# Two-layer masked GNN on one core: layer 1's query and key weights multiplied with the map's on the chip, and part of a round's products moved into the next round

## The chip, the core and the metric

One core of a Trainium2 chip. TensorE multiplies into PSUM, VectorE and ScalarE take results out of PSUM, GpSimd works in SBUF, SyncE (SP) issues most DMAs. The metric is the device time of one execution in microseconds. The kernel before: 4122.58 us, median of 3 runs (4117.27 to 4124.95).

## The reference, cut to what matters

x has the shape (64, 256, 512): 64 graphs of 256 nodes; adj is a boolean mask (64, 256, 256). Graphs don't depend on each other.

```python
# layer 0: 4 heads of 64
h = maximum(layernorm(x), 0)
q, k, v = h @ Wq, h @ Wk, h @ Wv
x = x + softmax(where(adj, q @ k.T / 8, -max)) @ v @ Wo + bo
# layer 1: 8 heads of 64
h = maximum(layernorm(x), 0)
m = h @ map_w.T + map_b
q, k = m @ q_w.T + q_b, m @ k_w.T + k_b
n = m / norm(m per head)
cos_adj = (n @ n.T, zero where adj) > 0.1
p = softmax(where(adj, -1e10, q @ k.T / 8)) * keep
a = cos_adj * p
out = relu(a @ (h @ gcn_map.T + gcn_map_b) @ gcn_W.T / (a.sum(-1) + 1))
x = x + out
```

## The kernel before, in words

All is kept in SBUF for one graph at a time; weights are loaded once. Most products are made of three fp32r matmuls: each operand is held as a high part (rounded to fp32r) and a low part (the rest), and `PASSES` multiplies high by high, high by low and low by high. The high part is written by ScalarE from PSUM, the low part by VectorE (PSUM less the high part). Transposes, the products with attention weights and the sums of squares are plain fp32.

The work is software-pipelined over rounds. `rounds` calls a body with (a, n): in one round the heads' part of layer 1 of graph a, and all else for graph n = a + 1. The first round has only n, the last only a; 63 rounds have a new graph behind the first. The order of each engine inside a round is a written list, one per engine: `TENSOR`, `SCALAR`, `VECTOR`, `POOL`, `SYNC` (from L50 on). An engine runs its list strictly in order, with semaphore waits. Strings are steps of graph n, tuples (with a pair number 0 to 3) steps of graph a.

Steps of graph n: `ht0a/b` transposes h of layer 0 (hT high and low); `qk0` to `qk3` project q, k; `v0` projects v; `s0` to `s3` are scores of four heads, followed by exp on ScalarE, `sum` (GpSimd scales prob, L417); `pt` transposes prob; `av` multiplies with v; `wo0/1` is the output projection, after which VectorE makes x_mid and its statistics (L663, L533, L540), GpSimd rstd (L359, L362) and VectorE h (`norm1`, L546). `ht1a/b` transposes it. `m0` to `m3` are the map. ScalarE writes qkm high, VectorE m32 (L670) and qkm low (L671). `q0`..`q3` and `k0`..`k3` project q and k from qkm; `vv0/1` is the value product with a weight `w_v` which the kernel makes itself in the first round (`fold`: gcn_map times gcn_W). `ss` sums squares of m, GpSimd raises them to -1/2 (`pow`, L441), `rt` transposes and `bc0/1` spread them over partitions; VectorE scales m32 (L699).

Steps of graph a, for each pair of heads: `unit` (nrm high L518, low L402), `score`, `cos`, ScalarE's exp (L475), VectorE's mask and gate (L607, L618), `turn_a/b` (transposes to uT, L481), `value` (L783), `back` (transposes; VectorE L634, GpSimd adds to x_res, L410).

PSUM has 8 banks: 0 to 3 belong to the pairs' steps, 4 to 7 go round the string steps in TENSOR's order (`bank_of`). `empty` makes TensorE wait until the previous user of a bank has been taken out.

Of the kernel before, what the change touches and what calls it, by code (L numbers as in the profile page):

```python
# [23 lines left out]
def gnn_two_layers(nc, x, adj, wq, wk, wv, wo, bo, map_t, map_b, q_t, q_b, k_t, k_b, gcn_map, gcn_map_b, gcn_t, out):  # L24
# [3 lines left out]
    DH = 64  # L28
# [75 lines left out]
    with ctx:  # L104
# [28 lines left out]
        hT = sb("hT", [128, 2, KT, N], F32R)  # L133
        qkm = sb("qkm", [128, 2, KT, N], F32R)
# [7 lines left out]
        q1 = sb("q1", [128, 2, KT, N], F32R)  # L142
        k1 = sb("k1", [128, 2, KT, N], F32R)
# [7 lines left out]
        gcn_rows = att[:, :, :, :, :].rearrange("p a b c n -> p (a b c n)").rearrange("p (h d) -> p h d", d=D)  # L151
        rel = sb("rel", [128, C, 128])
# [43 lines left out]
        fold_done = count("fold_done")  # L196

# [8 lines left out]
        pT_ready = count("pT_ready")  # L206

# [67 lines left out]
        SPLIT_HIGH = at(SCALAR, ("qk0", "qk2", "exp0", "exp1", "pt0", "pt2"), 4)  # L275
        SPLIT_LOW = at(VECTOR, ("qk1", "qk3", "sum0", "sum1", "av", "wo0"), 4)
        FOLD = at(TENSOR, ("s2", "pt0", "av", "wo0", "ht1a"), 0)
        FOLD_HIGH = at(SCALAR, ("exp3", "pt1", "av", "ht1a"), 0)
        FOLD_LOW = at(VECTOR, ("sum3", "av", "wo0", "ht1a", "ht1b"), 0)
# [3 lines left out]
        def _(sp):  # L283
            with nc.allow_non_contiguous_dma("small biases, once"):
                sp.dma_start(x_in[:, :, :], x[0].rearrange("(c p) d -> p c d", p=128)).then_inc(x_loaded, 16)
                sp.dma_start(adj8[:, :, :], adj[0].rearrange("(c p) j -> p c j", p=128)).then_inc(adj_loaded, 16)
# [8 lines left out]

            def body(a, n, more):
                for s in steps(SYNC, a, n, more):
                    kind, p = s if isinstance(s, tuple) else (s, None)
                    if kind == "x":
# [5 lines left out]
                        sp.dma_start(x_in[:, :, :], x[n + 1].rearrange("(c p) d -> p c d", p=128)).then_inc(x_loaded, 16)  # L305
                    elif kind == "out":
# [4 lines left out]
                    elif kind == "move":  # L311
# [21 lines left out]
        def _(pool):  # L333
# [44 lines left out]
            def body(a, n, more):  # L378
                for s in steps(POOL, a, n, more):
# [66 lines left out]
        def _(act):  # L446
# [13 lines left out]
            def body(a, n, more):  # L460
                for s in steps(SCALAR, a, n, more):
# [3 lines left out]
                    if a is None and kind in FOLD_HIGH:  # L465
                        kt = FOLD_HIGH[kind]
                        act.wait_ge(fold_full, kt + 1)
                        s_.activation(w_v[:, 0, kt, :], bank[kt][:, :], ACT.Copy).then_inc(fold_hi, 1)
# [17 lines left out]
                    elif kind[:2] == "ht":  # L486
                        t = 2 * "ab".index(kind[3])
                        act.wait_ge(product_full, in_psum(n, kind))
                        s_.activation(flat(hT[:, 0, t:t + 2, :]), bank[bank_of[kind]][:, :], ACT.Relu).then_inc(high_done, 1)
# [19 lines left out]
                    elif kind[0] in "mqk" and kind[1].isdigit():  # L509
                        t = int(kind[1])  # L510
                        dst, bias = {"m": (qkm, bias_m), "q": (q1, bias_q), "k": (k1, bias_k)}[kind[0]]
# [3 lines left out]
                        s_.activation(dst[:, 0, t, :], bank[bank_of[kind]][:, 0:N], ACT.Identity, bias=bias[:, t:t + 1]).then_inc(high_done, 1)  # L515
# [4 lines left out]
            rounds(act, body)  # L520

        @block.vector
        def _(dve):
# [404 lines left out]
```

## Time and profile before

| | |
|---|---|
| median of 3 runs | 4122.58 us |
| profiled execution, its own time | 4121.26 us |
| its span, first to last instruction | 4119.5 us |
| TensorE matmul busy | 3931.4 us, 95% |
| TensorE weight loads | 3437.0 us, 83% |
| VectorE / ScalarE / GpSimd busy | 63% / 48% / 32% |
| mean granted TensorE clock | 0.993 of full |
| the chain that ended last | TensorE 65%, VectorE 12%, issue 11%, ScalarE 6%, GpSimd 4% |

How to read it: busy time of TensorE overlaps itself, since matmuls are pipelined and their ends are modelled; times from one group's start to the next one's start are surer. A fp32 matmul is listed as two records, a transpose as one. "Idle before" names what ended the idle time ahead of an instruction.

### The profile page before, as it was taken

How to read it: one execution, taken by the hardware profiler on the slowest of the kernel's cores; microseconds unless marked ns; L12 is line 12 of the kernel's file. 1: busy time of each engine (PE TensorE's matmuls, PEld its weight loads, DVE VectorE, ACT ScalarE, POOL GpSimd, SP SyncE). 2: the span in 40 equal slices, each digit the busy share in tenths (PEclk: the TensorE clock that was granted, in tenths of full speed). 3: DMA queues.
4: the chain of work that ended last, by engine and by line, in shares of the span. 5: the costliest groups of instructions: out<-in, count | busy, mean ns of one | idle time of the engine just before them, and what ended most of it. 6: DMA issues, size and time to landing. Idle time of an engine off the chain costs nothing.

```text
span 4119.5 us, 105002 instructions
## 1 busy us (share of the span) xinstructions
PE 3931.4 (95%) x32976; PEld 3437.0 (83%) x32976; DVE 2608.3 (63%) x9426; ACT 1979.3 (48%) x5583; POOL 1324.3 (32%) x2007
## 2 busy tenths in 40 slices
PE   7999999999999999999999999999999999999997
PEld 6888888888888888888888888888888888888886
DVE  4666666666666666666666666666666666666664
ACT  3554544544545445445454454454454544544544
POOL 3333333333332333333333333333333333333332
PEclk8999999999999999999999999999999999999998
DMA  3000000000000000000000000000000000000000
GB/s 87 16 32 26 22 32 16 32 32 16 32 27 21 32 18 30 32 16 32 29 18 32 22 25 32 16 32 32 16 32 27 21 32 16 32 32 16 32 27 17
DMA packets 65544, 111.77 MB, mean 27 GB/s; under 512 B 20880, under 2 KB 22448, under 8 KB 65520
## 3 DMA queue, kind: packets, MB, share of 16 engines
q1 hardware_dynamic: 64928, 110.12, 7.8%
q0 software_dynamic: 592, 1.35, 0.2%
q8 instruction: 13, 0.21, 0.0%
q14 instruction: 11, 0.09, 0.0%
HBM read 44.34 MB, written 33.55 MB: 19 GB/s over the span
## 4 chain that ended last, share of the span: by engine, by line
PE 65%; DVE 12%; issue 11%; ACT 6%; POOL 4%; DVEq 1%; DMA 1%; POOLq 0%; ACTq 0%; SPq 0%
PE bank L755 34%; PE bank L763 9%; PE bank L748 7%; PE bank L783 6%; PE bank L775 4%; ACT prob L501 3%; PE bank L883 3%; POOL prob L417 2%; DVE x_mid L663 2%; ACT att L475 2%; DVE prob L650 2%; DVE att L607 2%; DVE att L618 1%; POOL rstd L362 1%; DVE hT L640 1%
## 5 line engine op out<-in xcount | busy, mean ns | idle before, releaser
L475 ACT ACTIVATE att<-att,nmax 128x256 f32<-128x256 f32 x1024 | 509.7, 500 | 299.6 <-DVE nmax L607 299.6
L417 POOL TENSOR_SCALAR prob<-prob,rsum 128x256 f32<-128x256 f32 x512 | 241.1, 487 | 631.2 <-DVE rsum L657 628.2
L755 PE MATMUL bank<-hT,w_qkv 128*128 128x256 f32 x3072 | 414.9, 288 | 4.7 <-DVE hT L640 4.7
L755 PE MATMUL bank<-qkm,w_k 128*128 128x256 f32 x3072 | 416.6, 285 | 0.0
L755 PEld LDWEIGHTS bank<-hT,w_qkv 128*128 128x128 f32 x3072 | 376.9, 189 | 37.9 <-issue 24.2
L755 PE MATMUL bank<-hT,w_map 128*128 128x256 f32 x3072 | 396.7, 285 | 5.1 <-DVE hT L640 1.0
L618 DVE SCALAR_TENSOR_TENSOR att<-bank,att 128x256 f32<-128x256 f32 x1024 | 392.3, 420 | 4.0
L755 PE MATMUL bank<-qkm,w_q 128*128 128x256 f32 x3072 | 390.8, 283 | 0.0
L755 PEld LDWEIGHTS bank<-hT,w_map 128*128 128x128 f32 x3072 | 372.5, 189 | 18.4 <-DVE hT L640 17.3
L763 PE MATMUL bank<-w_v,hT 128*128 128x512 f32 x1536 | 385.3, 399 | 0.0
L755 PEld LDWEIGHTS bank<-qkm,w_k 128*128 128x128 f32 x3072 | 380.1, 188 | 5.0
L481 ACT ACTIVATE uT<-bank 128x512 f32<-128x512 f32 x512 | 292.2, 598 | 181.1 <-PE bank L748 169.5
L515 ACT ACTIVATE q<-bank,bias_q 128x256 fp32r<-128x256 f32 x256 | 121.0, 473 | 537.1 <-PE bank L755 535.2
L607 DVE CUSTOM_DVE_ANT_0 att<-bank,mask 128x256 f32<-128x256 f32 x1024 | 372.1, 420 | 7.3 <-PE bank L775 2.3
L755 PEld LDWEIGHTS bank<-qkm,w_q 128*128 128x128 f32 x3072 | 373.4, 189 | 0.1
L763 PEld LDWEIGHTS bank<-w_v,hT 128*128 128x128 f32 x1536 | 278.6, 188 | 82.6 <-issue 24.2
L783 PE MATMUL bank<-uT,v 128*64 128x256 f32 x2048 | 280.1, 395 | 49.4 <-ACT uT L481 49.4
L410 POOL TENSOR_TENSOR x_res<-x_res,rel 128x256 f32<-128x256 f32 x256 | 189.0, 738 | 420.4 <-DVE rel L634 420.4
L689 DVE SCALAR_TENSOR_TENSOR q<-bank,bias_q,q 128x256 fp32r<-128x256 f32 x256 | 117.1, 478 | 321.4 <-ACT q L515 321.4
L359 POOL TENSOR_SCALAR var_e<-mv 128x2 f32<-128x2 f32 x128 | 24.7, 193 | 913.9 <-DVE mv L540 913.9
L634 DVE SCALAR_TENSOR_TENSOR rel<-bank,fac 128x256 f32<-128x256 f32 x256 | 108.7, 424 | 314.6 <-PE bank L820 310.1
L515 ACT ACTIVATE k<-bank,bias_k 128x256 fp32r<-128x256 f32 x256 | 121.5, 474 | 373.9 <-PE bank L755 373.9
(122 smaller groups left out, 7949.6 us busy)
## 6 DMA issues: line engine op xcount, KB each, us to landing
x_in<-x SPq DMA_DIRECT2D x64, 512.0 KB, 3.4
x_res<-x_mid SPq DMA_DIRECT2D x64, 512.0 KB, 3.1
out<-x_res SPq DMA_DIRECT2D x64, 512.0 KB, 2.8
adj<-adj SPq DMA_DIRECT2D x64, 64.0 KB, 2.6
att<-gcn_map POOLq DMA_DIRECT2D x2, 512.0 KB, 9.0
x_mid<-wq SPq DMA_DIRECT2D x1, 512.0 KB, 5.6
x_res<-wk SPq DMA_DIRECT2D x1, 512.0 KB, 6.8
v<-wv SPq DMA_DIRECT2D x1, 512.0 KB, 7.7
```

The costliest lines, as they stand in the source:

```text
L410: g.tensor_tensor(part, part, rel[:, :, :], ALU.add).then_inc(res_added, 1)
L417: last = g.tensor_scalar(prob0[:, hd, c, :], prob0[:, hd, c, :], rsum0[:, hd, c:c + 1], 0.0, ALU.mult, ALU.add)
L475: s_.activation(e_sl, e_sl, ACT.Exp, bias=nmax1[:, p, c, e:e + 1], scale=-1.0, accum_out=esum1[:, p, c, e:e + 1]).then_inc(exp1_done, 1)
L481: s_.activation(uT[:, e, :], t_bank[e][:, :], ACT.Copy).then_inc(uT_ready, 1)
L515: s_.activation(dst[:, 0, t, :], bank[bank_of[kind]][:, 0:N], ACT.Identity, bias=bias[:, t:t + 1]).then_inc(high_done, 1)
L607: v_.tensor_tensor_reduce(out=att[:, p % 2, e, c, :], in0=score_bank[e][:, c * N:c * N + N], in1=mask1[:, c, :], scale=-SCALE, scalar=FLT_ ...
L618: v_.scalar_tensor_tensor(e_sl, gram_bank[e][:, c * N:c * N + N], COS_THRESHOLD, e_sl, ALU.is_gt, ALU.mult, accum_out=usum1[:, p, c, e:e + ...
L748: last = t_.transpose(dst[:, b * 128:b * 128 + 128], src_of(outer, c), ident[:, :])
L755: last = t_.matmul(dst, w(ws, k)[:, t * 128:t * 128 + 128], rhs[:, rs, k, :], start=(k == 0 and i == 0), stop=(k == KT - 1 and i == 2))
L763: last = t_.matmul(dst, lhs[:, ls, k, c * 128:c * 128 + 128], w(ws, k), start=(k == 0 and i == 0), stop=(k == chunks - 1 and i == 2))
L775: last[e] = t_.matmul(banks[e][:, c * N:c * N + N], left[r, ls, c * 128:c * 128 + 128], right[r, rs, :], start=(i == 0), stop=(i == 2))
L783: last = t_.matmul(dst[64 * e:64 * e + 64, :], v[:, jc, (hd0 + e) * DH:(hd0 + e + 1) * DH], rhs(e, jc), start=(jc == 0), stop=(jc == C - 1))
```

## The change

1. q and k of layer 1 no longer come from m but from h directly: in the first round the kernel multiplies q_t and k_t with the map's weights (8 folds of 4 fp32 matmuls of 128x512) and their bias (2 folds of 16 matmuls of one column), takes the results out as high and low parts, and adds the bias. The raw weights (`q_raw`, `k_raw`, `map_raw`) are loaded to slots that are free then. The value weight's folds stay.
2. m is only needed in fp32: ScalarE writes m32, VectorE has no operation for m.
3. `q`, `k` of pairs 2 and 3 and both value products are made in the next round, as steps of graph a: `("k", 2)`, `("q", 2)`, `("k", 3)`, `("q", 3)`, `("vv", 0)`, `("vv", 1)`. q1, k1 hold two pairs in place of four.
4. The transposed h of layer 1 has a buffer of its own, gT, as it must live into the next round.
5. All five orders are written anew. `empty` now knows products of both kinds.

```diff
     TENSOR = [
-        "ht0a", ("score", 0), "ht0b", ("cos", 0), "qk0", "qk1", ("turn_a", 0), "qk2", ("turn_b", 0), "s0", "s1", ("value", 0),
-        "qk3", ("back", 0), ("score", 1), ("cos", 1), "s2", "s3", "pt0", "v0", "pt1", ("turn_a", 1), ("turn_b", 1), "pt2",
-        "pt3", ("value", 1), "av", ("back", 1), ("score", 2), ("cos", 2), "wo0", "wo1", ("turn_a", 2), ("turn_b", 2),
-        ("value", 2), ("score", 3), ("back", 2), "ht1a", "ht1b", ("cos", 3), "m0", "m1", "m2", ("turn_a", 3), ("turn_b", 3),
-        "m3", ("value", 3), "vv0", "ss", "q2", "q1", "q0", "k1", ("back", 3), "rt", "k0", "q3", "k3", "bc0", "bc1", "k2",
-        "vv1"
+        ("vv", 0), "ht0a", ("score", 0), ("cos", 0), ("vv", 1), ("turn_a", 0), "ht0b", ("k", 2), ("turn_b", 0), "qk0",
+        ("value", 0), ("score", 1), "qk1", "qk2", "qk3", ("back", 0), "s0", "s1", ("cos", 1), "s2", "s3", "v0", "pt0",
+        ("turn_a", 1), ("turn_b", 1), "pt1", "pt2", ("q", 2), "pt3", ("value", 1), "av", ("back", 1), ("score", 2), ("cos", 2),
+        "wo0", "wo1", ("k", 3), ("turn_a", 2), ("turn_b", 2), ("q", 3), ("value", 2), "ht1a", "ht1b", ("back", 2),
+        ("score", 3), ("cos", 3), "m0", "m1", "m2", "m3", "q0", ("turn_a", 3), "ss", ("turn_b", 3), "k0", ("value", 3), "rt",
+        "q1", "bc1", "bc0", "k1", ("back", 3)
     ]
...
     VECTOR = [
...
+        ("vv", 0), ("score_a", 0), "ht0a", ("score_b", 0), ("cos_a", 0), ("cos_b", 0), "ht0b", ("vv", 1), ("factor", 0),
+        ("score_a", 1), "qk0", ("k", 2), ("score_b", 1), "qk1", "qk2", ("back", 0), "qk3", "s0", ("cos_a", 1), "s1", "sum0",
+        "s2", ("cos_b", 1), "sum1", "s3", "sum2", "v0", "sum3", ("q", 2), ("factor", 1), ("back", 1), "av", ("score_a", 2),
+        ("score_b", 2), ("cos_a", 2), "wo0", ("cos_b", 2), "wo1", ("k", 3), "norm1", ("factor", 2), ("q", 3), ("back", 2),
+        "ht1a", "ht1b", "stats0", ("score_a", 3), ("score_b", 3), ("cos_a", 3), ("cos_b", 3), "ss", "q0", "k0", "rt", "norm0",
+        ("factor", 3), "bc0", "q1", ("back", 3), "bc1", "k1"
     ]
     POOL = [
...
+        ("unit", 0), ("unit", 1), "mid", "mask0", ("back", 0), "sum0", "sum1", "sum2", "sum3", ("back", 1), "rstd1",
+        ("back", 2), "rstd0", "m0", "m1", "m2", "m3", "pow", "mask1", ("back", 3)
     ]
     SYNC = [
-        "x", ("out", 0), "move", "adj"
+        "x", ("out", 0), "adj", "move"
     ]
...
-        q1 = sb("q1", [128, 2, KT, N], F32R)
-        k1 = sb("k1", [128, 2, KT, N], F32R)
+        q1 = sb("q1", [128, 2, 2, N], F32R)
+        k1 = sb("k1", [128, 2, 2, N], F32R)
...
+        gT = sb("gT", [128, 2, KT, N], F32R)
...
-                    elif kind in ("m0", "m1", "m2", "m3"):
-                        t = int(kind[1])
-                        v_.tensor_scalar(m32[:, t, :], full[:, 0:N], bias_m[:, t:t + 1], None, ALU.add)
-                        v_.scalar_tensor_tensor(qkm[:, 1, t, :], full[:, 0:N], bias_m[:, t:t + 1], qkm[:, 0, t, :].bitcast(F32),
-                                                ALU.add, ALU.subtract).then_inc(product_done, 1)
...
+                if f in (BIAS_Q, BIAS_K):
...
+                    for t in range(KT):
+                        for k in range(KT):
+                            last = t_.matmul(full[:, t:t + 1], raw(k)[:, t * 128:t * 128 + 128], bias_m[:, k:k + 1], start=(k == 0), stop=(k == KT - 1))
+                else:
+                    t = f - (QUERY_W if query else KEY_W)[0]
+                    for k in range(KT):
+                        last = t_.matmul(full[:, :], map_raw[:, k, t * 128:t * 128 + 128], raw(k), start=(k == 0), stop=(k == KT - 1))
...
+                    if kind in ("q", "k", "vv"):
+                        pe.wait_ge(product_done, out_of_psum(a, "ht1b"))
+                        empty(a, n, s)
+                        if kind == "vv":
+                            last = project_rows(full[:, :], gT, KT, p, lambda s2, k: w_v[:, s2, k, :])
                         else:
-                            pe.wait_ge(stage_lo, {"qk0": 3, "wo0": 4, "m0": 6, "q0": 8, "k0": 10}[kind])
+                            w = {"q": w_q, "k": w_k}[kind]
+                            last = project(full[:, 0:N], lambda s2, k: w[:, s2, k, :], p, gT)
```

In the first round the folds stand in TensorE's order ahead of these steps: folds 0, 1 at s2; 2, 3 at pt0; 4 at av; 5 (bias of q) and 6 at ht1a; 7 at m0; 8 at m1; 9 at m2; 10 (bias of k) to 14 at m3. The second half of `k_raw` is loaded once fold 9 is full. q_t and k_t are no longer split into high and low parts.

## Rows read from the trace of the kernel before

**Rows 1.** Stages: us, busy time (instructions) of each engine, granted clock, DMA, GB/s
```profile
1990.63:2053.80 63.17, 60.93 (x516) 53.32 (x515) 40.53 (x147) 30.70 (x87) 20.52 (x32) 1.00 0.07 26
0.00:96.12 96.12, 68.10 (x426) 62.05 (x427) 43.26 (x90) 30.20 (x57) 27.08 (x51) 0.86 0.31 87
4077.93:4119.50 41.57, 24.73 (x169) 15.88 (x168) 16.12 (x81) 15.04 (x45) 5.21 (x6) 0.70 0.04 13
```
**Rows 2.** Timeline of TensorE, one round: start, us, line, operands, count, idle before
```profile
1990.63 0.60 PE L748 MATMUL bank<-ident,h 128*128 128x128 f32 x4
...
2008.81 1.04 PE L748 MATMUL bank<-ident,att 128*128 128x128 f32 x8
2009.68 1.33 PE L748 MATMUL bank<-ident,prob 128*128 128x128 f32 x8
2010.95 1.08 PE L783 MATMUL bank<-uT,v 128*64 128x256 f32 x8
...
2018.60 1.04 PE L748 MATMUL bank<-ident,att 128*128 128x128 f32 x8
2020.37 1.08 PE L783 MATMUL bank<-uT,v 128*64 128x256 f32 x8 [0.74 <-ACT uT L481]
...
2022.29 0.44 PE L820 MATMUL bank<-ident,oT 128*128 128x128 f32 x2
2024.09 1.09 PE L748 MATMUL bank<-ident,h 128*128 128x128 f32 x8 [1.36 <-DVE h L546]
...
2033.92 3.06 PE L763 MATMUL bank<-w_v,hT 128*128 128x512 f32 x12
2036.83 1.84 PE L883 MATMUL bank<-half_of,ptm 128*128 128x2 f32 x16
2038.53 4.50 PE L755 MATMUL bank<-qkm,w_q 128*128 128x256 f32 x36
2042.87 1.58 PE L755 MATMUL bank<-qkm,w_k 128*128 128x256 f32 x12
...
2044.50 0.38 PE L889 MATMUL bank<-ident,rn 128*8 128x128 f32 x2
...
2053.80 0.60 PE L748 MATMUL bank<-ident,h 128*128 128x128 f32 x4
```
**Rows 3.** Waits of TensorE: who waited for whom, us in total, times, longest
```profile
PE bank L748 <- DVE h L546: 93.6, 64, 8.3
PE bank L783 <- ACT uT L481: 49.4, 67, 0.8
```
**Rows 4.** Groups by form in 2000 to 2063.17: count, busy us, mean ns, idle before
```profile
L671 DVE SCALAR_TENSOR_TENSOR qkm<-bank,bias_m,qkm 128x256 fp32r<-128x256 f32 x4 | 1.9, 476 | 0.0
L441 POOL TENSOR_TENSOR rn<-ssq,minus_half 128x16 f32<-128x16 f32 x1 | 2.9, 2902 | 2.9 <-DVE ssq L692 2.9
L424 POOL TENSOR_TENSOR ptm<-ptm 128x256 f32<-128x256 f32 x4 | 2.4, 620 | 3.8 <-DVE qkm L671 3.8
L402 POOL TENSOR_TENSOR nrm<-ptm,nrm 128x512 fp32r<-128x512 f32 x2 | 2.6, 1282 | 5.3 <-ACT nrm L518 5.3
L699 DVE TENSOR_TENSOR ptm<-bank,ptm 128x512 f32<-128x512 f32 x2 | 1.3, 681 | 0.0
L518 ACT ACTIVATE nrm<-ptm 128x512 fp32r<-128x512 f32 x2 | 1.3, 628 | 1.1 <-DVE ptm L699 1.1
```
**Rows 5.** Timelines of VectorE and GpSimd around norm1
```profile
2020.91 0.41 DVE L540 BATCH_NORM_AGGREGATE mv<-stats 128x2 f32<-128x6 f32 x2
2022.64 1.40 DVE L546 TENSOR_SCALAR h<-x_mid,mv,rstd 128x512 f32<-128x512 f32 x2 [1.32 <-POOL rstd L362]
2022.57 0.73 POOL L410 TENSOR_TENSOR x_res<-x_res,rel 128x256 f32<-128x256 f32 x1
```
**Rows 6.** Timeline of TensorE in the first round
```profile
34.97 1.65 PE L775 MATMUL bank<-qkm 64*128 64x256 f32 x12 [8.51 <-DVE qkm L644]
79.44 6.03 PE L755 MATMUL bank<-qkm,w_q 128*128 128x256 f32 x36
```

More of the change, by code:

```diff
@@ L21, with gnn_two_layers @@
 FLT_MAX = float(np.finfo(np.float32).max)
-def gnn_two_layers(nc, x, adj, wq, wk, wv, wo, bo, map_t, map_b, q_t, q_b, k_t, k_b, gcn_map, gcn_map_b, gcn_t, out):
+def gnn_two_layers(nc, x, adj, wq, wk, wv, wo, bo, map_t, map_rows, map_b, q_t, q_b, k_t, k_b, gcn_map, gcn_map_b, gcn_t, out):
     G, N, D = x.shape
@@ L61, in gnn_two_layers @@
-        ("turn_a", 1), ("turn_b", 1), "pt2", "pt3", ("value", 1), "av", ("exp_a", 2), ("exp_b", 2), ("turn_a", 2),
-        ("turn_b", 2), ("value", 2), "ht1a", "ht1b", ("exp_a", 3), "m0", ("exp_b", 3), "m1", ("turn_a", 3), "m2",
-        ("turn_b", 3), "m3", "q2", ("value", 3), "q1", "k1", "q0", "k0", "q3", "k3", "k2"
+        ("unit", 0), "ht0a", ("unit", 1), ("exp_a", 0), ("exp_b", 0), "ht0b", ("turn_a", 0), ("turn_b", 0), ("k", 2), "qk0",
+        ("exp_a", 1), "qk1", "qk2", ("value", 0), "qk3", ("exp_b", 1), "exp0", "exp1", "exp2", "exp3", "pt0", "pt1", "pt2",
@@ L64, in gnn_two_layers @@
+        ("turn_a", 1), ("turn_b", 1), ("q", 2), "pt3", ("value", 1), "av", ("exp_a", 2), ("exp_b", 2), ("turn_a", 2),
+        ("turn_b", 2), ("k", 3), ("q", 3), ("value", 2), "ht1a", "ht1b", ("exp_a", 3), "m0", ("exp_b", 3), "m1", "m2", "m3",
+        "q0", ("turn_a", 3), ("turn_b", 3), "k0", ("value", 3), "q1", "k1"
     ]
     VECTOR = [
-        "ht0a", "ht0b", ("score_a", 0), ("score_b", 0), ("cos_a", 0), "qk0", ("cos_b", 0), "qk1", "s0", "qk2", "s1",
-        ("factor", 0), "sum0", ("back", 0), "sum1", "qk3", ("score_a", 1), ("score_b", 1), "s2", ("cos_a", 1), "s3",
@@ L238, in gnn_two_layers, with rounds @@
         res_added = count("res_added")
-        def rounds(eng, body):
+        def rounds(eng, body, join=None):
             body(None, 0, True)
+            if join is not None:
+                join()
             with nc.Fori(0, G - 2, engines=[eng.engine], hint_back_edge=True) as a:
@@ L273, in at, with first, folded @@
             return {s: first + i for i, s in enumerate(s for s in order if s in names)}
[L275 to L279, printed above, removed]
+        SPLIT_HIGH = at(SCALAR, ("qk0", "qk2"), 4)
+        SPLIT_LOW = at(VECTOR, ("qk1", "qk3"), 4)
+        BIAS_V, BIAS_Q, BIAS_K = 4, 5, 10
+        VALUE_W, QUERY_W, KEY_W = range(0, 4), range(6, 10), range(11, 15)
+        FOLDS = 15
+        def first(order, names):
+            return next(s for s in order if s in names)
+        TAIL = ("q0", "k0", "q1", "k1", "vv0", "vv1")
+        FOLD = {"s2": (0, 1), "pt0": (2, 3), "av": (4,), "ht1a": (5, 6), "m0": (7,), "m1": (8,), "m2": (9,),
+                first(TENSOR, TAIL + ("m3",)): (10, 11, 12, 13, 14)}
+        FOLD_HIGH = {"exp2": (0,), "exp3": (1,), "pt1": (2,), "pt2": (3,), "m0": (6, 7), "m1": (8,), "m2": (9,),
+                     first(SCALAR, TAIL + ("m3",)): (11, 12, 13, 14)}
+        FOLD_LOW = {"sum2": (0, 1), "av": (2, 3), "wo0": (4,), "ht1b": (5,), first(VECTOR, TAIL + ("ss",)): (6, 7, 8, 9, 10, 11, 12, 13, 14)}
+        HIGH_FOLDS = [f for f in range(FOLDS) if f not in (BIAS_V, BIAS_Q, BIAS_K)]
+        def folded(f, half):
+            if f in VALUE_W:
+                return w_v[:, half, f, :]
+            return w_q[:, half, f - QUERY_W[0], :] if f in QUERY_W else w_k[:, half, f - KEY_W[0], :]
         block = ctx.enter_context(nc.Block())
@@ L711, in _ @@
             pe.sem_inc(o_full, PAIRS1)
-            def fold(kt):
-                if kt == 0:
-                    pe.wait_ge(pick_made, 3)
-                if kt == KT:
-                    pe.wait_ge(fold_done, KT)
-                for half in range(2):
-                    part = slice(64 * half, 64 * half + 64)
-                    for i in range(4):
-                        hd = 4 * half + i
-                        left = gcn_rows[part, i, kt * 128:kt * 128 + 128] if kt < KT else gcn_bb[part, i, :]
-                        last = t_.matmul(bank[kt % KT][:, hd * DH:hd * DH + DH], left, gcn_w[part, :], start=True, stop=True)
-                    if half == 0:
-                        last.then_inc(fold_half, 1)
-                        pe.wait_ge(fold_half, kt + 1)
-                last.then_inc(fold_full, 1)
```

278 lines of the change are left out of this document (201 added, 77 removed), and 3 rows, old and new, of the table VECTOR.

## The prediction, made before the changed kernel was run

> **What bounds the kernel now.** I read the stage table first: in one steady round (1990.63 to 2053.80) TensorE is busy 60.9 of 63.17 us at full granted clock, VectorE 40.5, ScalarE 30.7, GpSimd 20.5 [rows 1]. TensorE bounds, and no other engine comes near it by load. The starts of "ht0a" in two following rounds give the period, 63.17 us [rows 2]. Next the list of waits of TensorE: only two kinds are long in sum, 93.6 us behind VectorE's h and 49.4 us behind ScalarE's uT, each about once a round [rows 3]. Last the timeline of TensorE, group by group from start to next start, because "busy" hides waits under modelled ends. It shows three losses in a round [rows 2]:
> - 2018.60 to 2020.37: eight transposes take 1.77 us; the same eight at 2008.81 take 0.87. 0.90 us is a wait of "value 2" for uT.
> - 2022.29 to 2024.09: the two transposes of "back 2" (0.44 in their row, about 0.35 without the overlap) have 1.80 us. 1.45 us is a wait of "ht1a" for h.
> - 2009.68 to 2010.95: eight transposes of prob take 1.27, so 0.40 us is a wait for GpSimd's scaling of prob.
>
> Together 2.75 us. The other 60.42 us of the round are matmuls and weight loads back to back.
>
> **The change, part by part.**
> *TensorE's steady work: 0.* Before, q and k take four chunks by three passes from qkm; after, the same from gT. 96 projections of 128x256 before and after, 48 for m, 24 of 512 columns for vv. What shrinks is only the waits.
>
> *VectorE: -3.8 us a round, worth 0.* The split of m goes: four of L671 at 476 ns and four of L670 at about the same, 8 x 0.48 = 3.8 [rows 4]. VectorE had 22 us to spare; I count it at nothing, but it lets evictions come earlier. ScalarE keeps four operations for m (they now write m32), GpSimd keeps its squares.
>
> *The wait at "value 2" (0.90): gone.* "k3" now stands ahead of the transposes of pair 2, "q3" between them and "value 2". Twelve projections take 1.45 us (36 in 2038.53 to 2042.87, 4.34) [rows 2]; 1.45 covers 0.90. The cover gone, the 0.90 comes back.
>
> *The wait at "ht1a" (1.45): down to 0.4.* Between the end of "wo1" (2018.60) and "ht1a" (2024.09) lie 5.49 us. This is a chain: eviction, statistics, mv done 2021.32, var_e and rstd on GpSimd, then h, 2022.64 to 2024.04 [rows 2, 5]. After, TensorE has k3 1.45 + transposes 0.87 + q3 1.45 + value 2 1.05 = 4.8 us there. h takes 1.40 us beside GpSimd's x_res addition at 2022.57 [rows 5]; "back 2" now follows, so h may take less, 1.0 as my estimate (its two passes without the third of overlap). The chain is then 5.1 to 5.2: 0.4 is left. If VectorE's queue (k3's eviction now stands ahead of h, and waits for ScalarE's, behind both uT copies) adds to it, all of it comes on top.
>
> *The wait in the softmax of layer 0 (0.40): gone.* s2, s3 start 0.9 + 0.85 us behind s0, and between s2 and "pt3" now lie v0, the transposes of pair 1 and q2: 0.85 + 2.9 + 4 x 0.44 + 0.44 + 1.45 = 7.4 us, before 6.2. By hand the last scaled prob is ready about 0.8 us ahead.
>
> *A new wait at "rt": +0.6.* Before, ss ended at 2038.53 and rt started at 2044.50; 6 us of q and k stood between. The chain inside is ssq, 0.2, and GpSimd's pow of 128x16, 2.90 [rows 4], with hand-overs of 0.1 each about 3.5 us. Behind ss there are now one pair half 0.43, k0 1.45 and value 3 1.05 = 2.9. So 0.6 us of wait.
>
> *The norm chain into "cos 0": covered.* From m3 to cos 0: eviction 0.6, square 0.62, ss 1.70, pow 3.5, rt 0.15, two copies 1.2, bc 0.25, scale 0.7, nrm high 0.63, nrm low 1.27 [rows 2, 4], with hand-overs 11.3 us. TensorE has q0, ss, two pair halves, k0, value 3, 0.6 wait, q1, bc, k1, back 3 = 10.9, then vv0 2.9 (12 in 2033.92 to 2036.83), ht0a 0.5, score 0 0.9: 15.2 us. By queue order GpSimd can't start nrm low before "back 3" is through (10.9 + 0.2 + 0.4 + 0.1 + 0.75 = 12.35), so it ends at 13.7: room 1.5.
>
> *The rest moved.* k2 (ahead of turn b of pair 0) and vv1 (behind cos 0) stand where VectorE and ScalarE work on scores; I find "qk0" covered by only 0.2 us behind ht0b. SP's "adj" goes ahead of "move": its condition (mask1) is met before "out" can be, so the move to x_res waits for nothing new, and "mid" needs it 8 us later than it lands. gT takes away the reuse of hT; no wait of TensorE hung on it.
>
> Period after: 60.42 + 0.4 + 0.6 = **61.4 us**, 1.77 less. 63 rounds run behind the first: -111.5 us.
>
> *Once, first round.* Eight folds of four 128x512 fp32 matmuls and two bias folds. The nearest rows: value 2 has 8 records for 4 written matmuls of 256 columns in 1.08 us, 0.27 each [rows 2]. If its two heads do not overlap, 512 columns cost 0.54 and 32 of them 17 us; if they overlap, 1.08 and 34 us. I take 27: a transpose of 128 fp32 columns costs 0.109, twice that over four times the columns is 0.87. The bias folds: ss has 16 records for 8 matmuls in 1.70, 0.21 each; 32 make 6.8. Sum 34, with 2 us for the second half of k_raw (its load is issued when fold 9 is full) and 1.7 for the last eviction: 38.
> Against it: k2, k3, q2, q3, vv0, vv1 leave the first round, 4 x 1.45 + 2 x 2.9 = 11.6. The stall of 8.51 us ahead of s2 goes, since VectorE no longer splits q_t there [rows 6]. The two bias folds (6.8) stand in the norm chain of 5.5, which was idle. TensorE is busy in 68.1 of the 96.12 us, at 0.86 of the clock [rows 1]; 36 projections take 6.03 us there and 4.50 in a steady round [rows 2, 6], a third more. If two thirds of the busy time came to the steady rate, 68.1 x 2/3 x 1/4 is 11; I take 10 for what denser work wins back. 96.1 + 38 - 11.6 - 8.5 - 4 - 10 = 100: **+4**, bounds -8 and +15.
>
> *Once, at the end.* The last graph alone takes 41.57 us with TensorE busy 24.7 at 0.70 [rows 1]. It now has the 11.6 us too, most of it inside waits of the pair steps: **+2.5**, bounds 0 and +8.
>
> Sum: 4119.5 - 111.5 + 6.5 = 4014.5 us of span; the profiled execution lies 1.8 above its span (4121.26), so 4016; it is 1.3 under the median shown. Forecast **4016 us**.
>
> **Two places of the skill.** The row says 8 records for 4 matmuls, and leaves open whether heads overlap. The Trainium skill (FP8 and Floating Point Precision, on true FP32) says four passes go through the array; by it, at the clock granted, a fold matmul would be 0.85 us, 27 us in all, and the lower bound of 17 falls.
> h took 1.40 us with GpSimd's addition starting beside it [rows 5]. The Trainium skill (SBUF - State Buffer, on the shared port pair) says one engine fully blocks the other when VectorE is in a 2-port mode, tensor_scalar among them. By it norm0, now near mask1 and back 3, could lose 0.4 to 0.7 ahead of bc; the room of 1.5 holds it, so the sum stays.
>
> **Rivals.**
> A, forecast: period 61.1 to 61.7; 3997 to 4035. Chance 0.45.
> B, all waits filled: neither rt nor ht1a waits, as the evictions find a less loaded VectorE. Period 60.4 to 61.1 (by the same sum 3953 to 3997), about 60.8, 63 x 0.6 = 38 less: 3978. For it: 3.8 us less on VectorE. Against: pow's 2.90 us can't shrink. 0.17.
> C, the in-order queues give back half: h behind k3's eviction, ht0b, or the bunched s0 to s3 (VectorE, ScalarE and GpSimd each have four heads at 0.7 to 1.0 us in a row). Each costs 0.2 to 0.9; period 61.7 to 63, about 62.3, 63 x 0.9 = 57 more: 4073. 0.28.
> D, slower: nrm low. GpSimd takes it only behind mask1 and back 3, VectorE's bc0 only behind norm0 and factor 3, which waits for cos b of pair 3. Once this is late by more than its room of 1.5 us TensorE stands at cos 0 each round; from 3.3 us the gain is gone. At 4 us late: period 63.9, 4121 + 46 + 6.5 = 4174. For it: before, 22.9 us of TensorE lay between m3 and cos 0, now 15.2. Against: chain and queues add to 13.7. 0.05.
> E, the change gains only what the first round costs (period 63.05 to 63.1, 4119.5 - 6 + 6.5 + 1.8 = 4122): within 0.2% of before, 0.05. This is also where it would not do what it says: q3 and k3 in the waits, but the waits' ends moved along by them.
>
> **How the numbers follow.** What can be told from no change is 0.2%, 8 us. A, B and C hold 0.90: faster. E 0.04 to same; D and a part of E 0.06 slower. Range: from B's middle to just above C's, 3978 to 4078; it leaves out the low end of B, the upper part of C, D and E, about 0.2. It takes in the unknown cost of the folds (-8 to +15).
>
> **What would show it.** Period by two starts of ht0a: 61.4. Waits of TensorE for h under 0.5 us a round, for uT at value 2 none, a new one of 0.6 at rt behind GpSimd's pow; cos 0 without a wait. The first ht0a of the second round at 100 + 3 us. A fold matmul 0.85 us. VectorE 3.8 us a round less. Wrong is the forecast if TensorE waits at cos 0, at qk0 or at pt over 0.3 us a round, or h moves back with wo1.

## The result: 3965.8 us, below the predicted range

| | before | after |
|---|---|---|
| median (4 runs each) | 4123.24 us | 3965.78 us |
| lowest to highest | 4117.27 to 4124.95 | 3964.82 to 3967.96 |
| ratio | | 0.9621, 95% interval 0.9605 to 0.9638 |
| span of the profiled execution | 4119.5 us | 3963.0 us |

The forecast was 4016 us with a range of 3978 to 4078. The sign was right, and the gain was 157 us where 107 had been worked out. The next sections split it, show which term was wrong, and which runs say so. One execution of run 9 below took 6799.7 us at a mean granted clock of 0.752 and is left out of every comparison.

First the stage windows of the changed kernel, which answer to [rows 1]: start:end, length, then busy us of TensorE (with its records), of its weight loads, VectorE, ScalarE and GpSimd, granted clock, DMA share and GB/s. The first line is one steady round, the second the first round, the third the end.

```profile
2000.00:2060.33 60.33, 59.80 (x517) 53.17 (x516) 37.14 (x140) 31.03 (x87) 20.69 (x31) 1.00 0.08 27
0.00:116.22 116.22, 90.92 (x483) 68.97 (x483) 38.93 (x82) 27.53 (x55) 26.37 (x50) 0.90 0.28 79
3917.02:3963.00 45.98, 31.78 (x243) 24.87 (x241) 19.83 (x89) 17.81 (x51) 6.16 (x7) 0.89 0.09 35
```

A steady round is (3917.02 - 116.22) / 63 = 60.33 us, before (4077.93 - 96.12) / 63 = 63.20 [rows 1]. So 63 x 2.87 = 181 us came from the steady rounds; the first round gave back 20.1 and the end 4.4. Together -156.5, the difference of the spans.

Waits of TensorE, the two that answer to [rows 3] (us in all, times, longest; the 8.3 is one wait in the first round):

```profile
PE bank L1055 <- POOL rn L505: 21.8, 64, 1.7
PE bank L902 <- DVE h L638: 21.6, 64, 8.3
```

The wait for h fell from 93.6 to 21.6 us, the one of the matmuls for uT from 49.4 (67 waits) to 1.4 (2 waits), and a new one at "rt" sums to 21.8.

The timeline of TensorE, parts of one round, against [rows 2]: start, us, line, operands, count, idle before.

```profile
1985.46 3.04 PE L917 MATMUL bank<-w_v,gT 128*128 128x512 f32 x12
1988.34 0.60 PE L902 MATMUL bank<-ident,h 128*128 128x128 f32 x4
1988.87 0.97 PE L929 MATMUL bank<-k,q 64*128 64x256 f32 x12
1989.67 0.87 PE L929 MATMUL bank<-nrm 64*128 64x256 f32 x12
1990.48 3.07 PE L917 MATMUL bank<-w_v,gT 128*128 128x512 f32 x12
...
2021.38 1.58 PE L909 MATMUL bank<-gT,w_k 128*128 128x256 f32 x12
2022.80 1.03 PE L902 MATMUL bank<-ident,att 128*128 128x128 f32 x8
2023.59 1.66 PE L909 MATMUL bank<-gT,w_q 128*128 128x256 f32 x12
2025.18 1.08 PE L937 MATMUL bank<-uT,v 128*64 128x256 f32 x8
2026.48 1.09 PE L902 MATMUL bank<-ident,h 128*128 128x128 f32 x8 [0.21 <-DVE h L638]
...
2037.01 1.84 PE L1049 MATMUL bank<-half_of,ptm 128*128 128x2 f32 x16
2038.71 0.63 PE L902 MATMUL bank<-ident,att 128*128 128x128 f32 x4
2039.10 1.66 PE L909 MATMUL bank<-gT,w_k 128*128 128x256 f32 x12
2040.69 1.08 PE L937 MATMUL bank<-uT,v 128*64 128x256 f32 x8
2042.10 0.38 PE L1055 MATMUL bank<-ident,rn 128*8 128x128 f32 x2 [0.32 <-POOL rn L505]
...
2049.97 0.87 PE L929 MATMUL bank<-nrm 64*128 64x256 f32 x12
```

Read from start to next start, as in the forecast. "value 2" at 2025.18 starts 1.59 us after q3 and waits for nothing. "ht1a" starts 1.30 us after "value 2", where 1.01 does without a wait (run 9 below has 1.02 for the same eight records): 0.29 is left of 1.45. "rt" starts 1.41 us after "value 3": 0.40 of wait. "cos 0" at 2049.97 has none.

Single operations, which answer to [rows 4, 5]: h of norm1 on VectorE, the power and the last product of the norm chain on GpSimd.

```profile
2025.35 1.00 DVE L638 TENSOR_SCALAR h<-x_mid,mv,rstd 128x512 f32<-128x512 f32 x2
2039.14 2.90 POOL L505 TENSOR_TENSOR rn<-ssq,minus_half 128x16 f32<-128x16 f32 x1 [2.63 <-DVE ssq L801]
2047.31 1.29 POOL L466 TENSOR_TENSOR nrm<-ptm,nrm 128x512 fp32r<-128x512 f32 x1
```

The records of ss end at 2038.85; the power starts at 2039.14 and ends at 2042.04, 0.06 ahead of rt. The last nrm ends at 2048.60; cos 0 starts at 2049.97, so it has 1.4 us of room.

The first round of the changed kernel, TensorE, against [rows 6]:

```profile
16.69 7.82 PE L909 MATMUL bank<-hT,w_qkv 128*128 128x256 f32 x48 [6.44 <-DVE hT L756]
26.88 0.98 PE L929 MATMUL bank<-qkm 64*128 64x256 f32 x12 [2.37 <-DVE qkm L760]
30.37 6.29 PE L836 MATMUL bank<-gcn_w,att 64*128 64x64 f32 x29 [2.52 <-DVE v L685]
...
83.78 0.58 PE L854 MATMUL bank<-bias_m,v 128*128 128x1 f32 x4 [2.14 <-DMA x_res<-k_t]
...
88.76 3.76 PE L858 MATMUL bank<-v,att 128*128 128x512 f32 x4
...
94.19 1.88 PE L858 MATMUL bank<-v,att 128*128 128x512 f32 x4
...
97.63 1.88 PE L858 MATMUL bank<-v,att 128*128 128x512 f32 x4
...
112.68 0.38 PE L1055 MATMUL bank<-ident,rn 128*8 128x128 f32 x2 [1.72 <-POOL rn L505]
```

From 94.19 to 97.63 are 8 records, that is 4 written matmuls of 128x512: 3.44 us, 0.86 each, 27.5 us for 32 at full clock. The records at 88.76 take twice that: the granted clock stands at its lower level, 1.2 GHz. It fell from 85.56 on, in the middle of the one-column matmuls that follow the wait of 2.14 us:

```profile
85.56:88.76 3.20, 3.20 (x18) 3.20 (x18) 0.00 (x0) 0.00 (x0) 0.00 (x0) 0.54 0.00 0
88.76:92.32 3.56, 3.56 (x6) 1.49 (x7) 0.16 (x1) 0.00 (x0) 0.00 (x0) 0.50 0.00 0
```

The first fold of q behind its bias fold, 60.84 to 66.06, ran at 0.71 and 0.64, and no wait stood directly ahead of it.

### The profile page after: what moved, and what is told of

Its sections match the earlier page's. It is cut to its first block and busy times, and to the rows that moved or that the text cites. A ratio compares the mean times of both kernels' runs of the same rounds, so it can differ in the third digit from the quotient of the medians.

```text
span 3963.0 us, 104587 instructions
## 1 busy us (share of the span) xinstructions
PE 3888.6 (98%) x33104; PEld 3442.2 (87%) x33104; DVE 2387.8 (60%) x8920; ACT 1999.5 (50%) x5587; POOL 1333.9 (34%) x2007
## 5 line engine op out<-in xcount | busy, mean ns | idle before, releaser
L909 PE MATMUL bank<-gT,w_q 128*128 128x256 f32 x3072 | 421.7, 286 | 0.0
L909 PE MATMUL bank<-gT,w_k 128*128 128x256 f32 x3072 | 415.7, 284 | 0.0
L917 PE MATMUL bank<-w_v,gT 128*128 128x512 f32 x1536 | 390.7, 403 | 0.0
L909 PEld LDWEIGHTS bank<-gT,w_k 128*128 128x128 f32 x3072 | 384.6, 189 | 6.0
L909 PEld LDWEIGHTS bank<-gT,w_q 128*128 128x128 f32 x3072 | 381.2, 189 | 1.6 <-DVE w_k L661 0.2
L909 PE MATMUL bank<-gT,w_map 128*128 128x256 f32 x3072 | 382.3, 284 | 0.1
L909 PEld LDWEIGHTS bank<-gT,w_map 128*128 128x128 f32 x3072 | 367.6, 188 | 10.6 <-issue 2.2
L917 PEld LDWEIGHTS bank<-w_v,gT 128*128 128x128 f32 x1536 | 278.3, 188 | 66.5
L593 ACT ACTIVATE prob<-prob,nmax 128x256 f32<-128x256 f32 x512 | 255.4, 500 | 86.3 <-DVE nmax L766 86.2
L902 PE MATMUL bank<-ident,att 128*128 128x128 f32 x2048 | 289.4, 274 | 3.1 <-DVE att L733 3.0
```

The source lines that it names most:

```text
L593: last = s_.activation(prob0[:, hd, c, :], prob0[:, hd, c, :], ACT.Exp, bias=nmax0[:, hd, c:c + 1], scale=-1.0, accum_out=esum0[:, hd, c:c ...
L902: last = t_.transpose(dst[:, b * 128:b * 128 + 128], src_of(outer, c), ident[:, :])
L909: last = t_.matmul(dst, w(ws, k)[:, t * 128:t * 128 + 128], rhs[:, rs, k, :], start=(k == 0 and i == 0), stop=(k == KT - 1 and i == 2))
L917: last = t_.matmul(dst, lhs[:, ls, k, c * 128:c * 128 + 128], w(ws, k), start=(k == 0 and i == 0), stop=(k == chunks - 1 and i == 2))
```

## Experiments

"Period" is the spacing of two powers of the norm (GpSimd, rn<-ssq), one in each round: before 63.14 in most rounds (mean 63.23), after 60.30 (mean 60.33). It doesn't depend on the first round or the end. Runs 1 to 8 are one execution each, runs 9 and 10 medians of several. All times stand beside runs of the kernel before on the same chip, which took 4119 to 4131 us.

**1. The fold alone.** The changed kernel with the five orders of before, four slots for q1 and k1, gT = hT; m32 still comes from ScalarE alone.

```diff
-        gT = sb("gT", [128, 2, KT, N], F32R)
+        gT = hT
-        q1 = sb("q1", [128, 2, 2, N], F32R)
+        q1 = sb("q1", [128, 2, KT, N], F32R)
```

> The changed kernel with the orders of before: weights folded, q and k projected from h, no split of m on VectorE, but all products in their own round, in the old places. Theory M (the moved products and the new orders fill the waits): the waits at value 2 (0.9 us) and at ht1a (1.45 us) stay, period 62.9 to 63.2 us; the folds lengthen the start, the whole is slower than before, near 4130 us. Rival F (the fold itself brings it, by a freer VectorE and no wait of q, k for m): period near 60.5, the whole near 3975 us.

4151.4 us (before 4122.0), period 63.17. Its waits are those of [rows 3]:

```profile
PE bank L896 <- DVE h L634: 93.7, 64, 8.3
PE bank L931 <- ACT uT L568: 49.4, 67, 0.8
```

So q and k from h, and VectorE's relief from the split of m, bring nothing in a round by themselves. They cost 30 us once (span 4149.6 against 4119.5). The gain is in the moved work and the new orders. It does not need the fold: runs 4 and 5 move only q and k of pairs 2 and 3, without it, and are 84 and 124 us faster than the kernel before.

**2. The split of m put back.** VectorE writes m32 and the low part of m again, in the changed order (m0 between the cosine halves of pair 3 in its list, m1 to m3 ahead of ss).

```diff
-  s_.activation(m32[:, t, :], bank[bank_of[kind]][:, 0:N], ACT.Identity, bias=bias_m[:, t:t + 1]).then_inc(m_ready, 1)
+  s_.activation(mT[:, 0, t, :], bank[bank_of[kind]][:, 0:N], ACT.Identity, bias=bias_m[:, t:t + 1]).then_inc(mh_done, 1)
...
+  v_.tensor_scalar(m32[:, t, :], full[:, 0:N], bias_m[:, t:t + 1], None, ALU.add)
+  v_.scalar_tensor_tensor(mT[:, 1, t, :], full[:, 0:N], bias_m[:, t:t + 1], mT[:, 0, t, :].bitcast(F32), ...
```

> The changed kernel, in which VectorE again writes m32 and the low part of m and ScalarE the high part, as before (the split is written and never read): 3.8 us a round more on VectorE, squares and the bank's release wait for VectorE. Theory M: period 60.3 to 60.6, as VectorE has 24 us to spare; at most ss and rt come 0.3 us later. Rival F: a good part of the 2.87 us a round comes back, period over 61.3.

4039.9 us, most rounds 61.43, mean 61.52: theory M had at most 60.6, rival F's "over 61.3" came out. A wait stands where there was none, at "ss" (line 1061 here):

```profile
PE bank L1061 <- POOL ptm L491: 43.6, 64, 0.7
...
2013.04 1.95 PE L1061 MATMUL bank<-half_of,ptm 128*128 128x2 f32 x16 [0.69 <-POOL ptm L491]
```

VectorE is 3 us busier a round and far from full, 40 of 61.4 us. But m's chain is longer by its turn in VectorE's queue, the squares come 0.7 us late, and ss, rt and the rest of the chain with them. From turn a of pair 3 to ss it is 1.29 us (2011.75 to 2013.04), in the changed kernel 0.44: 0.85 of the 1.1. What VectorE gave up is worth nothing in the old order (run 1) and 1.1 us in most rounds of the new one (1.19 by the mean, 75 us in all; the time is 74 us up).

**3. The filler earlier.** k3 and q3 ahead of wo0, not around the transposes of pair 2; the other engines' orders follow.

```diff
-        "wo0", "wo1", ("k", 3), ("turn_a", 2), ("turn_b", 2), ("q", 3), ("value", 2), "ht1a", "ht1b", ("back", 2),
+        ("k", 3), ("q", 3), "wo0", "wo1", ("turn_a", 2), ("turn_b", 2), ("value", 2), "ht1a", "ht1b", ("back", 2),
```

> The changed kernel with k and q of pair 3 made ahead of wo0 in place of around the transposes of pair 2, nothing else. Theory M: the cover is gone, the wait for uT (0.7 to 0.9) is back at value 2, and h is awaited for 5.1 - 0.87 - 0.9 - 1.0 = 2.3 us; together 3.0 less the 0.3 that stands there now: period 62.9 to 63.1. Rival S (the gain comes from shorter switches and small waits all over the round, not from these two places): period under 61.5.

4163.7 us, slower than before. Both waits are back, and 29 of 63 rounds take 62.59, 2.3 us more than in the changed kernel, as the waits say (0.90 and 1.41 from start to start) and a little less than expected. The other 34 take 64.08. Two timelines at the same place, first (2 rows) a round of 62.59, then one of 64.08:

```profile
2003.35 1.08 PE L937 MATMUL bank<-uT,v 128*64 128x256 f32 x8 [0.74 <-ACT uT L570]
2006.06 1.09 PE L902 MATMUL bank<-ident,h 128*128 128x128 f32 x8 [1.63 <-DVE h L638]
...
2571.21 1.08 PE L937 MATMUL bank<-uT,v 128*64 128x256 f32 x8 [0.74 <-ACT uT L570]
2573.92 1.97 PE L902 MATMUL bank<-ident,h 128*128 128x128 f32 x8 [1.63 <-DVE h L638]
2575.68 0.64 PE L983 MATMUL bank<-ident,oT 128*128 128x128 f32 x2
2576.24 1.29 PE L929 MATMUL bank<-k,q 64*128 64x256 f32 x12
```

The waits are the same, but the eight transposes behind them take 1.97 against 1.09 us: the granted clock is at its lower level, 1.2 GHz, for most of this stretch. The windows over the same work have it at 0.65 against 1.00:

```profile
2006.06:2008.94 2.88, 2.88 (x34) 2.58 (x34) 1.79 (x5) 1.09 (x2) 0.74 (x1) 1.00 0.00 0
2573.92:2578.18 4.26, 4.26 (x35) 3.79 (x35) 2.08 (x6) 1.19 (x2) 0.74 (x1) 0.65 0.00 0
```

In the kernel before the two waits were 0.74 and 1.36 us, with score 3 and back 2 between them too, and the granted clock was 1.00 in 62 of the 63 rounds and 0.97 in the last. The two projections in between are worth the two waits, and here also the clock. Why 29 rounds with the same waits keep it stays open.

**4. No fold of q and k.** m is split into a buffer of its own, q and k of pairs 2 and 3 move, the value products stay in their own round, orders by hand.

```diff
-         gT = sb("gT", [128, 2, KT, N], F32R)
+         gT = hT
+         mT = sb("mT", [128, 2, KT, N], F32R)
-         FOLDS = 15
+         FOLDS = 5
-    ("vv", 0), "ht0a", ("score", 0), ("cos", 0), ("vv", 1), ("turn_a", 0), "ht0b", ("k", 2), ("turn_b", 0), "qk0",
+    "ht0a", ("score", 0), "ht0b", ("cos", 0), ("k", 2), "qk0", ("turn_a", 0), "qk1", ("turn_b", 0), "qk2",
...
```

> No fold of the query and key weights: q and k come from m as before, m split by ScalarE and VectorE into a buffer of its own; only q and k of pairs 2 and 3 move to the next round, vv0 and vv1 stay; orders written for that by hand. Theory M: the waits are filled as well, period 60.3 to 60.9, and the first round has no 34 us of folds, so it ends near 98: the whole 3945 to 3980 us, no worse than the changed kernel. Rival F: period over 62, the whole over 4045.

4037.8 us, period 62.00: rival F's bound for the period, but under its 4045 for the whole. Waits of my order: 44.1 us in all at bc (0.70 a round), 20.1 for layer 0's q and k at s2 (0.32), 29.0 for h. The first power runs at 74.83 against 109.72 us: the folds and what hangs on them cost 35 us once.

**5. The same with the order mended**, so that these waits go:

```diff
-    "ht0a", ("score", 0), "ht0b", ("cos", 0), ("k", 2), "qk0", ("turn_a", 0), "qk1", ("turn_b", 0), "qk2",
+    "ht0a", "ht0b", ("score", 0), ("cos", 0), ("k", 2), "qk0", ("turn_a", 0), ("turn_b", 0), "qk1",
...
-    "q1", "rt", "k1", "bc0", "bc1", "vv1"
+    "rt", "q1", "k1", "bc0", "bc1", "vv1"
```

(The first pair of lines is TensorE's order, the second VectorE's.)

> The version without the fold of q and k, orders mended: rt ahead of q1 on VectorE (its wait of 0.70 us at bc goes), qk2 and qk3 side by side and taken out ahead of back 0 (0.4 at s2 goes), ht0a and ht0b side by side (0.3). Theory M: period 61.99 - 1.4 = 60.6, the first round as short as without the fold: the whole 3940 to 3960, under the changed kernel's. Rival F: the split of m keeps it over 61.4, the whole over 4000.

4000.8 us, period 61.50, first power at 72.04. The round is 0.5 us shorter where 1.4 were expected, and both of rival F's bounds are just passed; but none of the waits that are left is for m or its squares. The wait at s2 is gone and 0.30 is left at bc, but a new 0.35 stands ahead of ht0b, whose PSUM bank VectorE still reads. Against the changed kernel it has 38 us less up to the first power, 1.23 x 63 = 78 more in the rounds and 4 less behind the last power: 36 us more in all. Against the kernel before it is 124 us faster, without any fold of q and k. Whether another order without folds reaches 60.3 stays open.

**6. Scores and cosine products apart.** The forecast had 60.42 us of TensorE work as given. The changed kernel has score and cos of pairs 0 and 3 next to each other; here one group of 128-row products stands between them; in the kernel before they stood apart too (ht0b, and back 2 with ht1a/b).

```diff
-        ("vv", 0), "ht0a", ("score", 0), ("cos", 0), ("vv", 1), ...
+        ("vv", 0), ("score", 0), "ht0a", ("cos", 0), ("vv", 1), ...
-        ("score", 3), ("cos", 3), "m0", "m1", "m2", "m3", ...
+        ("score", 3), "m0", ("cos", 3), "m1", "m2", "m3", ...
```

> The changed kernel with ht0a set between score 0 and cos 0, and m0 between score 3 and cos 3; no product, wait or engine's other order changes. Theory G (part of the gain is grouping: a run of 64-row products that follows 128-row ones starts about 0.1 us late each time): two more such starts and two more ends, period 60.50 to 60.80. Rival N (the rest of the gain is only waits gone): 60.3 as it was.

4031.7 us, period 61.39, 1.09 longer and more than expected, in part because m0 now waits 0.27 in each round for the low part of gT. The head of the round has no such wait:

```profile
2020.17 0.98 PE L929 MATMUL bank<-k,q 64*128 64x256 f32 x12
2021.08 0.66 PE L902 MATMUL bank<-ident,h 128*128 128x128 f32 x4
2021.66 0.97 PE L929 MATMUL bank<-nrm 64*128 64x256 f32 x12
2022.56 3.07 PE L917 MATMUL bank<-w_v,gT 128*128 128x512 f32 x12
```

From vv0 to vv1 it takes 5.37 us (2017.19 to 2022.56), in the changed kernel 5.02 (1985.46 to 1990.48), with the same 40 records of matmuls and transposes and no wait in either. The score group takes 0.91 where the transposes follow and 0.80 where the cos group does.

The second place, from score 3 to q0, can be read too once the wait is taken off:

```profile
1998.43 0.98 PE L929 MATMUL bank<-k,q 64*128 64x256 f32 x12
1999.68 1.69 PE L909 MATMUL bank<-gT,w_map 128*128 128x256 f32 x12 [0.27 <-DVE gT L756]
2001.31 0.98 PE L929 MATMUL bank<-nrm 64*128 64x256 f32 x12
2002.21 4.53 PE L909 MATMUL bank<-gT,w_map 128*128 128x256 f32 x36
2006.58 1.58 PE L909 MATMUL bank<-gT,w_q 128*128 128x256 f32 x12
```

It takes 8.15 us, in the changed kernel 7.43 (2027.72 to 2035.15). Score 3 has 1.25 to itself where 0.90 does without a wait, so 0.35 of the 0.72 is the wait and 0.37 is left. Head 0.35, wait 0.35 and 0.37 are 1.07 of the 1.09.

**7. The same move in the kernel before.**

```diff
-        "ht0a", ("score", 0), "ht0b", ("cos", 0), "qk0", ...
+        "ht0a", "ht0b", ("score", 0), ("cos", 0), "qk0", ...
```

> The kernel before with only one thing changed in TensorE's order: ht0a, ht0b, score 0, cos 0 in place of ht0a, score 0, ht0b, cos 0. Theory G: the four groups take 2.93 us there and 2.5 in the changed kernel's way of standing, so the period falls from 63.15 to 62.8 +- 0.1 and the whole to near 4100. Rival N: no change, 63.15.

4138.1 us, period 63.36, 0.2 longer, not shorter. Score and cos together do take less, 1.63 against 1.82 us. But ht0b now asks for a PSUM bank that VectorE has not emptied:

```profile
1998.25 0.66 PE L748 MATMUL bank<-ident,h 128*128 128x128 f32 x4 [0.35 <-DVE v L685]
```

From ht0a to qk0 it is 3.16 us (1997.31 to 2000.47), in the kernel before 2.93 (1990.63 to 1993.56). ht0a has 0.94 to itself; four transposes that another such group follows without a wait have 0.35 in the changed kernel (1993.82 to 1994.17). So the wait costs 0.59 and the grouping saves 0.36. The saving is in this run; the move is not worth it there.

**8. "rt" later, behind q1.**

```diff
-        ... ("value", 3), "rt", "q1", "bc1", "bc0", "k1", ("back", 3)
+        ... ("value", 3), "q1", "rt", "k1", "bc0", "bc1", ("back", 3)
```

> The changed kernel with q1 ahead of rt, then rt, k1, bc0, bc1 (VectorE: rt ahead of q1's eviction). If the wait of 0.4 us at rt is only GpSimd's power of 2.90 us being uncovered, it goes, and the period is 59.9 to 60.0, the whole near 3942. Rival: the chain into cos 0 then has no cover left, and the 0.4 us or more comes back as a wait at cos 0 or bc0: 60.3 or more.

4037.3 us, period 61.31. The wait at rt is gone, and a longer one is there:

```profile
2025.27 3.06 PE L917 MATMUL bank<-w_v,gT 128*128 128x512 f32 x12 [0.91 <-DVE ptm L808]
```

vv0 of the next round uses the PSUM bank of bc0, and VectorE empties it 0.91 us late. The rival on record was right that the wait comes back longer; it had it at cos 0 or bc0, and it stands at vv0.

**9. "ss" earlier.** The other side of the same wait: ss directly behind q0, ahead of the transposes of pair 3. And once, the second half of the key weight is loaded early, to a place free by then, so that the bias fold doesn't wait for it.

```diff
-        "m3", "q0", ("turn_a", 3), "ss", ("turn_b", 3), "k0", ("value", 3), "rt",
+        "m3", "q0", "ss", ("turn_a", 3), ("turn_b", 3), "k0", ("value", 3), "rt",
-        k_raw = [slots[k].rearrange("p (k d) -> p k d", d=D) for k in (2, 1)]
+        k_raw = [t.rearrange("p (k d) -> p k d", d=D) for t in (slots[2], prob0[:, 0:2, :, :].rearrange("p h c n -> p (h c n)"))]
```

> The changed kernel with two edits: ss stands ahead of both transposes of pair 3, so that GpSimd's power of 2.90 us has 0.44 us more cover; and the second half of the key weight goes to prob0's space as soon as fold 4 is done, so that it is not awaited. Theory: the wait at rt goes from 0.4 to under 0.1 a round, period 59.95 to 60.05 (-20 us); the 2.1 us of wait at the bias fold and the half clock behind it (some 3 us) go from the first round: the whole near 3942. Rival: ss then waits for GpSimd's square of m3 as long as it waited at rt, period 60.3; the whole near 3961.

3942.8 us, the median of 3941.4, 3942.8 and 3950.0; ratio 0.9567 to before (0.9547 to 0.9587). Period 60.06, close to the 59.95 to 60.05 of the theory. The place that waited:

```profile
2027.08 1.08 PE L937 MATMUL bank<-uT,v 128*64 128x256 f32 x8
2028.10 0.38 PE L1055 MATMUL bank<-ident,rn 128*8 128x128 f32 x2
```

Value 3 to rt is 1.02, and the list of waits has one wait for rn left, 1.7 us in the first round. The period fell by 0.25 and not by 0.40; ss takes 1.80 us behind q0 where it took 1.70. vv0 of the second round starts at 110.06 us. It is the fastest version run.

**10. The changed kernel again, on the same chip as run 9.**

> The changed kernel as it is, once more on this chip, to stand beside e10: 3963 to 3968, period 60.33; the end of its first round may move by some us with the arrival of the weights.

3965.4 us (3962.9 to 3969.9), ratio 0.9616 (0.96 to 0.9632), period 60.30, vv0 of the second round at 115.23. So run 9 is 22.6 us faster by the medians. By the profiled spans it is 22.7 (3963.7 against 3941.0): (60.325 - 60.08) x 63 = 15.4 in the rounds, 5.2 in the first, 2.1 at the end.

## Why the prediction was wrong, and where it was right

**The step that failed: "The other 60.42 us of the round are matmuls and weight loads back to back."** With the waits of 0.29 and 0.40 taken off, a changed round is 60.33 - 0.69 = 59.64 us. This is 0.78 less than the floor of the forecast, 49 us over 63 rounds. The forecast of "TensorE's steady work: 0" was right by count and wrong in time. The number of matmuls is the same; [rows 1] has 516 records of TensorE in a round and the changed kernel 517. What differs is what stands next to what. Between groups, the sums from start to next start went, in us a round: score and cos 6.93 to 6.52, layer 0's scores 1.79 to 1.65, the transposes ht0 1.11 to 0.88 and ht1 1.03 to 0.93, m 5.95 to 5.78, the backs down 0.13; q and k up 0.33, vv up 0.07, prob's transposes with their value products up 0.15 without their wait. Together -0.63 of the -0.78.

For two places this is shown: run 6 gave back 0.35 us a round by setting score 0 and cos 0 apart, with no wait in between, and 0.37 by setting score 3 and cos 3 apart, with the wait taken off. Run 7 saved 0.36 in the kernel before by bringing score 0 and cos 0 together. For the other groups, whose changes go both ways, there are only the sums. Each of the three moves adds or takes away two changes between matmuls with 128 rows of weights and those with 64, so all three fit a price of about 0.18 us for one change, an estimate (0.35 / 2). Nothing was run that measures it alone.

**VectorE, "worth 0".** Right in the old order and wrong in the new one. VectorE is 3.4 us less busy in a round (40.53 to 37.14), forecast 3.8. Run 1 has 0 in the old one; run 2 has 1.1 us in the new. The forecast looked for VectorE's load, not for its place in the chain m, squares, ss, power, rt. It did not move the sum, as the chain after rt was worked out with m from ScalarE.

**The waits.** "value 2": gone, as said, and run 3 brings it back. "ht1a": 0.29 against 0.4. h took 1.00 and not 1.40 us once GpSimd's addition no longer stood beside it; 1.0 was the estimate. The Trainium skill (SBUF - State Buffer, on the shared port pair) has the two engines exclude each other, and by it the time alone is the shorter. The two rows agree in this, but not in size: GpSimd's addition ran 0.66 us into h (2022.64 to 2023.30 [rows 5]), and h took 0.40 longer. Softmax of layer 0: gone, as said. "rt": 0.40 against 0.6, the same mechanism (2.90 us of power behind ss). "cos 0": no wait and 1.4 us of room against 1.5, so rival D had no ground. Both sizes of waits together are 0.31 a round to the good; this and the floor make -1.09, 63 x 1.09 = 69 us.

**The first round.** +20.1 against +4. The folds were sized right: 0.86 us for a matmul, and about 40 us for all that was called 38, as part ran at the lower clock. The 27 us for the 32 matmuls was a choice between bounds of 17 and 34; it measured 27.5 at full clock. The Trainium skill (FP8 and Floating Point Precision, on true FP32) has four passes, by which the forecast had estimated 0.85; the trace agrees; the lower bound of 17 us is out. What failed are the credits. Run 1 has the folds in and no step moved: its second round starts at 123.83 us, before at 96.12, so +27.7, where the same terms in the forecast (38 - 8.5 - 4 - 10) make 15.5. Moving the steps then took 7.6 us away (123.83 to 116.22) and not 11.6: the wait of 1.72 at rt is new, and its waits in the first 31 us, behind the first transposes, add to 11.3 against 7.2 in run 1. "-8.5, the stall goes": it came back as 6.44, 2.37 and 2.52, 11.3 us of waits against 13.5 (4.68 + 0.33 + 8.51) in the same stretch before. VectorE's splitting of q_t had stood there; what TensorE waited for now was the low part of hT, of q and k, and v. That these were late by the loads is argued from ScalarE's wait below, not shown. "-10, denser work": the granted clock rose from 0.86 only to 0.90, and the folds' own groups ran at the lower level for some 10 us (0.71 and 0.64 in 60.84 to 66.06, 0.54 and 0.50 in 85.56 to 92.32). "-4, bias folds in the idle norm chain": that of the key waited 2.14 us for its load, which is issued only when fold 9 is full; run 9 takes this wait away, and its first round is 5.2 us shorter than that of run 10.

**The end.** +4.4 against +2.5, inside its bounds.

The errors have opposite signs: -69 in the rounds (-49 the floor, -20 the waits), +16 in the first, +2 at the end, -51 in all: 4014.5 to 3963.0 of span. That the miss is as large as the error of the floor alone is luck, since the others cancel. Rival B, "all waits filled", held the measured time in its interval (3953 to 3997), in the low half that the stated range left out, but by another mechanism; both waits it did away with are there.

## What to carry to other kernels

Where one engine is full, its floor is not a constant: sum it from start to next start in the trace, group by group, and ask of a new order which groups become neighbours, since seams of some 0.18 us (an estimate), several of them a round, made 0.78 us where the sizes of the waits, argued to a tenth, were off by 0.31. Price relief of an engine that is not full by its place in a chain that a wait ends on, in the new order, not by its load. Of a credit for the first round ask what is late next; here the stall of 8.5 us had something nearly as late behind it. And test the moved work without the part that costs most: here the folds, without which 124 of the 157 us were there.

## What the runs showed of the chip that was not expected

- Behind two waits of 0.74 and 1.63 us (run 3) the granted clock went down in 34 of 63 rounds, 1.5 us each, and held in 29 with the same instructions around. Behind 0.74 and 1.36 us it held in 62 of the 63 rounds of the kernel before.
- GpSimd's power of 128x16 took 2.90 us, that of 128x2 0.71: 16 columns for 4.1 times the price of 2.
- Which PSUM bank a group gets can cost as much as an operand: 0.91 us a round in run 8, 0.35 in runs 5 and 7, each with the data long there.
- Loads of 512 KB at the start landed 12.8 us after issue for the map weights in the changed kernel, 10.2 for the first piece of q_t, and 3.3 for the second and for both of k_t, which were issued later. ScalarE stood 7.8 us for the former with the eviction of qk0 behind it.
